# Attention scores of a fused conv and attention layer: the product with k low as two 64-row matmuls in the row halves of TensorE

## The reference

```python
qkv = conv1d_same(group_norm(xf, gn_gamma, gn_beta), qkv_w, qkv_b)   # 16 taps, 256 -> 768 channels, 1024 positions
qkv = qkv.reshape(b * NUM_HEADS, -1, t)                              # 4 batches x 4 heads, 64 channels each for q, k, v
w = jnp.einsum('bct,bcs->bts', q * scale, k * scale)                 # scores, 1024 x 1024 per head
w = jax.nn.softmax(w.astype(jnp.float32), axis=-1)
h = jnp.einsum('bts,bcs->bct', w, v)
h = conv1d_same(h, proj_w, proj_b)                                   # 5 taps, 256 -> 256 channels
```

## Time and profile before

| what | value |
|---|---|
| median of 3 runs | 1116.28 us (1116.11 to 1116.67) |
| profiled execution, device time | 1117.09 us |
| its span | 1115.3 us |
| mean granted TensorE clock | 0.965 of full speed |
| PE busy | 1000.0 us, 90% |
| DVE, ACT, POOL busy | 64%, 58%, 21% |
| score matmuls (L1114) | 512 |

### The profile page before, as it was taken

The page is one execution under the profiler, slowest core; times in us unless marked ns, Lnnn a source line. Parts: engine busy times, 40 slices in busy tenths (PEclk is TensorE's granted clock), DMA queues, the critical chain, the costliest instruction groups (busy, mean ns, idle before and its releaser), DMA issues.

```text
span 1115.3 us, 18112 instructions
## 1 busy us (share of the span) xinstructions
PE 1000.0 (90%) x7250; PEld 716.3 (64%) x7250; DVE 717.4 (64%) x1222; ACT 650.3 (58%) x1049; POOL 233.2 (21%) x164
## 2 busy tenths in 40 slices
PE   2887749999999999999598999999999999988864
PEld 1555526667766777667366666766677668766654
DVE  5988557663765477668466555464636665777767
ACT  4674627664666477757565656465636575665531
POOL 2736112100230142124050100010001004313320
PEclk9998869999999999999799999999999999999978
DMA  7040034583459357637644384437435873453522
GB/s 269 21 170 1 1 124 77 95 200 67 95 105 246 54 120 167 161 60 161 153 76 86 66 172 100 81 72 181 82 65 124 184 170 68 96 123 60 112 57 76
DMA packets 284515, 122.59 MB, mean 110 GB/s; under 512 B 268304, under 2 KB 270736, under 8 KB 283536
## 3 DMA queue, kind: packets, MB, share of 16 engines
q1 hardware_dynamic: 284432, 121.44, 48.5%
HBM read 34.24 MB, written 15.87 MB: 45 GB/s over the span
## 4 chain that ended last, share of the span: by engine, by line
PE 63%; DVE 10%; issue 7%; ACT 6%; POOL 1%; DMA 1%; SPq 0%; ACTq 0%; POOLq 0%; DVEq 0%
PE cQ L1049 15%; PE cM L1049 15%; PE cP L1049 14%; PE psV L1095 8%; PE psS L1114 4%; PE psT L1114 4%; DVE smx L1491 2%; ACT arena L909 2%; DMA arena<-arena 1%; PE cM L990 1%; DVE W L1276 1%; PE cP L990 1%; DVE arena L1468 1%; DVE W L1362 1%; ACT arena L921 1%
## 5 line engine op out<-in xcount | busy, mean ns | idle before, releaser
L1049 PE MATMUL cP<-U,W 128*128 128x256 f16 (+1 forms) x1536 | 224.1, 303 | 13.6 <-DVE W L1276 12.1
L1049 PE MATMUL cM<-U,W 128*128 128x256 f16 (+1 forms) x1536 | 222.9, 301 | 11.4 <-DVE U L1305 7.4
L1049 PE MATMUL cQ<-U,W 128*128 128x256 f16 (+1 forms) x1536 | 226.7, 303 | 5.7 <-DVE W L1276 3.5
L1049 PEld LDWEIGHTS cP<-U,W 128*128 128x128 f16 x1536 | 150.6, 98 | 81.7 <-issue 11.6
L1049 PEld LDWEIGHTS cM<-U,W 128*128 128x128 f16 x1536 | 149.4, 97 | 80.7 <-issue 8.5
L1049 PEld LDWEIGHTS cQ<-U,W 128*128 128x128 f16 x1536 | 150.7, 98 | 73.4 <-issue 5.1
L1468 DVE SCALAR_TENSOR_TENSOR arena<-arena,smx 128x1024 f16<-128x1024 f32 x128 | 179.0, 1398 | 1.3 <-ACT arena L921 0.5
L902 ACT ACTIVATE smx<-smx,esc 128x1 f32<-128x1 f32 x128 | 37.5, 293 | 212.8 <-DVE smx L1491 212.5
L921 ACT ACTIVATE arena<-arena,smx 128x1024 f16<-128x1024 f32 x128 | 147.0, 1148 | 4.2
L1095 PE MATMUL psV<-arena 128*128 128x256 f16 x1024 | 125.2, 276 | 12.0 <-DVE arena L1475 6.2
L1491 DVE TENSOR_REDUCE smx<-psS 128x1 f32<-128x1024 f32 x64 | 77.9, 1218 | 76.2 <-PE psS L1114 75.9
(11 more groups left out here) (210 smaller groups left out, 1142.2 us busy)
## 6 DMA issues: line engine op xcount, KB each, us to landing
staging<-w_qkv SPq DMA_DIRECT2D x20, 512.0 KB, 5.2
kept_u<-U SPq DMA_DIRECT2D x4, 2077.0 KB, 9.9
U<-kept_u SPq DMA_DIRECT2D x16, 519.2 KB, 4.3
arena<-x_tok SPq DMA_DIRECT2D x8, 512.0 KB, 6.4
arena<-arena SPq DMA_DIRECT2D x16, 256.0 KB, 3.8
W<-x_tok SPq DMA_DIRECT2D x4, 1024.0 KB, 6.1
out_tok<-W SPq DMA_DIRECT2D x3, 1024.0 KB, 4.3
kept_h<-arena SPq DMA_DIRECT2D x4, 514.0 KB, 4.5
```

What stands on the lines that cost most here:

```text
L1049: last = mm(out, W[:, j, wl, c, wat + tap, :], U[:, slot, ul, c, at:at + width], start=(c == 0 and tap == 0 and wl + ul == 0), stop=(c == ...
```

## The change

The (q high + q low) x k low product is replaced by q high x k low alone; q low x k low is left out of the computation. For each unit the first two matmuls stay (128 rows, k high). The other two now take 64 rows each: the first half of the keys uses q high and k low in partitions 0 to 63, the second half uses a copy of q high and k low in partitions 64 to 127. They write different PSUM banks.

```diff
-        sizes = (3 * T, T, 2 * HALF, 2 * T, 3 * T, 4 * T, HR // 2)
+        sizes = (7 * HALF, T, HALF, 2 * T, 3 * T, 4 * T, HR // 2)
...
+        heads = part[0].bitcast(F16).rearrange("p (h w) -> p h w", h=2)
+        stack = heads[:, :, 0:2 * T].rearrange("p h (k t) -> p h k t", k=2)
+        k_low, q_again = heads[:, :, 2 * T:2 * T + HALF], heads[:, :, 2 * T + HALF:]
...
-        hbuf = part[2].rearrange("p (q t) -> p q t", q=2)
+        hbuf = part[2]
...
-                sp.wait_ge(S["qk_lo"], 2 * (2 * k + hd + 1))
-                sp.dma_start(stack[0:D, hd, 1:3, :].rearrange("p k t -> p (k t)"),
-                             stack[D:P, hd, 1:3, :].rearrange("p k t -> p (k t)")).then_inc(S["qk_done"], 16)
+                sp.wait_ge(S["qk_lo"], 3 * (2 * k + hd + 1))
+                sp.dma_start(stack[0:D, hd, 1, :], stack[D:P, hd, 1, :]).then_inc(S["qk_done"], 16)
+                sp.dma_start(q_again[D:P, hd, :], stack[0:D, hd, 0, :]).then_inc(S["qk_done"], 16)
...
                 act.wait_ge(S["pv_done"], 8 * k + 2 * gi + 2)
-                a(hbuf[R:R + D, 0, :], psV[O:O + D, :], ACT.Copy, scale=2.0 ** -PROB_BITS).then_inc(S["ht_done"], 1)
+                wait(act, "hl_done", 4 * k + gi)
+                a(hbuf[R:R + D, :], psV[O:O + D, :], ACT.Copy, scale=2.0 ** -PROB_BITS).then_inc(S["ht_done"], 1)
...
                         if u % 8 == 0:
-                            pe.wait_ge(S["qk_done"], 16 * (2 * k + hd + 1))
+                            pe.wait_ge(S["qk_done"], 32 * (2 * k + hd + 1))
...
+                        scores, queries = (psS, psT)[u % 2], slice(u % 8 * P, (u % 8 + 1) * P)
                         for h in range(2):
-                            for l in range(2):
-                                last = mm((psS, psT)[u % 2][:, h * HALF:(h + 1) * HALF], stack[:, hd, 0, u % 8 * P:(u % 8 + 1) * P],
-                                          stack[:, hd, 1 + l, h * HALF:(h + 1) * HALF], start=(l == 0), stop=(l == 1))
+                            mm(scores[:, h * HALF:(h + 1) * HALF], stack[:, hd, 0, queries],
+                               stack[:, hd, 1, h * HALF:(h + 1) * HALF], start=True, stop=False)
+                        mm(scores[:, 0:HALF], stack[0:D, hd, 0, queries], k_low[0:D, hd, :], start=False, stop=True)
+                        last = mm(scores[:, HALF:T], q_again[D:P, hd, queries], k_low[D:P, hd, :], start=False, stop=True)
                         last.then_inc(S["s_done"], 1)
...
-                    v.scalar_tensor_tensor(stack[D:P, hd, 2, :], yqk[D:P, :], ysc[D:P, m, 0:1], stack[D:P, hd, 1, :],
+                    v.scalar_tensor_tensor(k_low[0:D, hd, :], yqk[D:P, 0:HALF], ysc[D:P, m, 0:1], stack[D:P, hd, 1, 0:HALF],
+                                           ALU.mult, ALU.subtract).then_inc(S["qk_lo"], 1)
+                    v.scalar_tensor_tensor(k_low[D:P, hd, :], yqk[D:P, HALF:T], ysc[D:P, m, 0:1], stack[D:P, hd, 1, HALF:T],
                                            ALU.mult, ALU.subtract).then_inc(S["qk_lo"], 1)
```

More of the change, by code:

```diff
@@ L81, in build @@
         part = [arena[:, edge[q]:edge[q + 1]] for q in range(len(sizes))]
-        stack = part[0].bitcast(F16).rearrange("p (h k t) -> p h k t", h=2, k=3)
+        heads = part[0].bitcast(F16).rearrange("p (h w) -> p h w", h=2)
+        stack = heads[:, :, 0:2 * T].rearrange("p h (k t) -> p h k t", k=2)
+        k_low, q_again = heads[:, :, 2 * T:2 * T + HALF], heads[:, :, 2 * T + HALF:]
         vT = part[1].bitcast(F16).rearrange("p (s h c) -> p s h c", s=8, h=2)
-        hbuf = part[2].rearrange("p (q t) -> p q t", q=2)
+        hbuf = part[2]
         prob = part[3].rearrange("p (q t) -> p q t", q=2)
@@ L88, in build @@
         Hr = part[6].bitcast(F16).rearrange("p (l r w) -> p l r w", l=2, r=2)
-        xs = arena[:, 0:edge[2]].rearrange("p (n i c) -> p n i c", n=2, i=8)
+        xs = arena[:, 0:4 * T].rearrange("p (n i c) -> p n i c", n=2, i=8)
         EO = CT * 2 * SEQW
@@ L580, in add_common @@
                 else:
-                    wait(pool, "qk_lo", 2 * (2 * n + j - 1))
+                    wait(pool, "qk_lo", 3 * (2 * n + j - 1))
                 y = yv if j == 0 else yqk
@@ L803, in heads_hi @@
                     act.wait_ge(S["hr_free"], 16 * (k + 1))
-                a(home(k)[R:R + D, 0, r, 1:1 + HALF], hbuf[R:R + D, 1, :], ACT.Copy).then_inc(S["hh_done"], 1)
+                a(home(k)[R:R + D, 0, r, 1:1 + HALF], hbuf[R:R + D, :], ACT.Copy).then_inc(S["hh_done"], 1)
             def main_copy(n, p, j):
@@ L1474, in heads_sum @@
                 dve.wait_ge(S["ht_done"], 4 * k + gi + 1)
-                v.scalar_tensor_tensor(hbuf[R:R + D, 1, :], psV[R:R + D, :], 2.0 ** -PROB_BITS, hbuf[R:R + D, 0, :],
+                v.scalar_tensor_tensor(hbuf[R:R + D, :], psV[R:R + D, :], 2.0 ** -PROB_BITS, hbuf[R:R + D, :],
                                        ALU.mult, ALU.add).then_inc(S["hs_done"], 1)
@@ L1482, in heads_low @@
                 dve.wait_ge(S["hh_done"], 4 * k + gi + 1)
-                v.tensor_tensor(home(k)[R:R + D, 1, r, 1:1 + HALF], hbuf[R:R + D, 1, :],
+                v.tensor_tensor(home(k)[R:R + D, 1, r, 1:1 + HALF], hbuf[R:R + D, :],
                                 home(k)[R:R + D, 0, r, 1:1 + HALF], ALU.subtract).then_inc(S["hl_done"], 1)
```

## The result

| | before | after |
|---|---|---|
| device time, median of 15 runs each | 1116.67 us (1115.66 to 1117.39) | 1119.27 us (1118.82 to 1120.62) |
| ratio to before, 95% interval | | 1.0025 [1.0017, 1.0033] |
| span of the profiled execution | 1115.3 us | 1118.8 us |
| mean granted clock | 0.965 | 0.952 |

The change makes the kernel slower by 0.25%, 2.6 us, where 9.4 us of gain was forecast. The page reads almost as before: TensorE is busy 4.7 us longer and has 64% of the chain for 63%; where the time went, these totals don't say.

A forecast was written before the change was run, and what follows sets the result against it. TensorE was taken to bound 98 of 128 units: -10.3 us from pair and switches, +0.9 us for copies, -9.4 us against 1117.09 us gives 1107.7 us, as a median 1106.9, rounded 1107 us; range 1095 to 1133 us.

The forecast's parts named there:

- What bounds the kernel: Whole kernel: TensorE's time counts in 98 units of scores and not in 30, in step 4 and the last step.
- The pair: Each unit's two 64-row matmuls run at the same time, so four passes become three: 215 ns less per unit.
- The switch: Two changes per unit between 128-row and 64-row use, 55 ns each; a unit wins 105 ns, 98 units 10.3 us.
- rival A: TensorE, each unit: the switch is free, 21.1 us less plus 0.9 for the copies, 1096 us; chance 0.19.
- the case that I gave 0.09: TensorE's units: pair serial with free switches, or 100 to 115 ns per switch cancel the gain; 1115 to 1119 us.
- A full exposed tail, 164 ns: TensorE empties at both switches of each unit, 328 ns against 215 gained; 1128 us; chance 0.20.
- one with an exposed load beside it (262 ns): Each switch also exposes the weight load: a unit loses 309 ns, 1147 us; chance 0.16, shared with a serial pair.
- My other sign of being wrong: TensorE, each unit: the forecast is wrong if the unit takes longer than 0.86 us.
- The copies: SP issues two DMAs of 128 KB for one of 256 KB: one extra issue at the start, +0.9 us.
- DVE's split: k low's subtraction in two: +93 ns sixteen times, 1.5 us of DVE, at most +0.4 us exposed, counted as 0.
- The last step keeps its length: The last step, from 934 to 1066 us, should keep its length of some 110 us.
- Step 4's stall: TensorE's 11.5 us stall in step 4 should change little or grow by about a microsecond.

The follow-up runs named there:

- the second profile: The changed kernel profiled once more, unedited: 1119.51 us, ratio 1.0020.
- joined everywhere: Changed kernel with each even unit's scores from unit 2 on issued together with the next unit's, four full matmuls then two pairs: 1125.11 us, ratio 1.0074.
- joined where there was slack: Changed kernel with GpSimd's wait; units issued in twos except 4, 5, steps 4 and 8, and units 6, 7 of steps 2 and 3: 1109.81 us.

## Why the prediction was wrong

**What bounds the kernel** was read rightly for small changes: 0.22 us more per unit came back as 23.9 us for 98 units (21.6). For a gain of 0.4 us per unit it fails: the kernel without the pair gains nothing over step 3, where a wait for DVE comes up.

**The pair: right.** It saves one pass of 215 ns. Starts 10 ns apart, and a second pair for 0.22 us.

**The switch: the failed step.** I priced it at 55 ns, "a third of the tail", and said that this was a choice. It is 105 ns on average of the two changes. That a change costs something was right, the size not: 98 x (215 - 2 x 105), some 0.4 us, stands where the sum had 10.3. That alone is 9.9 of the 12.4 us between the forecast of 1106.9 and the 1119.27 measured. The nearest row that I leaned on, the float32 transposes, keeps all 128 rows in use, and so says nothing on a change of rows. I had noted that against rival A and should have held it against my own value too. The true value lies within the case that I gave 0.09 (100 to 115 ns cancel the gain), a nanosecond or two short of the 107 from which the change is slower by TensorE alone. A full exposed tail, 164 ns, is ruled out by the paces, and so is one with an exposed load beside it (262 ns). An exposed load in place of the tail, 98 ns, was no case of mine; it is near the measured price, and the sign that I had named for it, idle weight loads before L1119 and behind L1120, is there. My other sign of being wrong, a unit of more than 0.86 us, did not come, and the forecast fails all the same: at 0.85 us the gain is already gone, so the sign was set too far out. The Trainium skill, "TensorEngine Tiling (Array Packing)", section "Key Properties", says that a change of mode drains TensorE. The runs agree that each change costs and that staying in the mode doesn't; that the 100 ns are a drain no run here shows.

**The copies: too dear.** +0.9 us forecast, nothing measured: TensorE starts 0.1 us earlier in one profile and 0.1 us later in the other.

**DVE's split: the second failed step.** "I count 0, ... +0.4 us at most" was wrong by an order: the kernel before with the split alone takes 3.9 us more. Of the 3.2 us by which its profiled span grew, 2.3 came with the split's collisions and 0.9 with the late clock. I took the mean price of the instruction, 93 ns for the cut, and passed over the largest of the sixteen, 4031 ns, that stood in the same row. An instruction of 1285 ns that once takes 4031 waits there for something, and what waits once in one piece can wait twice in two. The additions of GpSimd that it meets are 4.5 us long, and two stand back to back. The Trainium skill, "SBUF — State Buffer", section "SBUF: two separate sides", has the rule: the port pair that DVE and GpSimd share is held exclusively for a whole instruction, and a DVE operation with two inputs in SBUF needs it against a GpSimd operation that reads SBUF. The runs agree: 0.75 us free, 3.50 and 4.87 us against two additions, and 0.48 us undisturbed with one input in PSUM.

**ACT's new wait: right,** it holds nothing. **The last step keeps its length: wrong,** by the split: from its first scores to the end of the span it takes 1.8 us more, and its last scores come 3.4 us later. **Step 4's stall: right** in size (11.84 us for 11.52), though the step as a whole grew by 1 us, by the same collision.

**The clock: not foreseen.** 1.3 us are lost in the profiled execution where the clock rises later behind the first copy (0.9 us in the second profile). Its cause is open, and that it comes from the change isn't shown.

**The sum as measured** by the lags of the profiled executions: +1.2 (first units, with the clock), -0.5 (the lag shrinks between the other places), +1.0 (step 4), +5.2 less 3.4 given back (last step), in all +3.5, the difference of the spans. The medians differ by less, 2.6 us: the profiled execution after was the slowest of its fifteen runs, 1.35 us above their median.

## What to carry to other kernels

Matmuls over half of the rows that run in pairs save a pass, but each change to them or back costs about half a pass of 512 columns here: they paid only where several pairs stood behind one another and the reordering made no new wait. When an instruction is to be cut in two, look at its longest record and not at its mean; if it waits for another engine's whole instruction there, each piece may wait for one. After a gain on the busiest engine, see slot by slot which wait comes next: joined everywhere, the units lost 5.8 us to new waits; joined where there was slack, and with GpSimd's collision gone (4.0 us by itself), they won 9.5 us over the changed kernel.

## What the runs showed of the hardware

- A change from 128-row to 64-row use and back costs 211 ns at the full clock, two times about 105; the weight load at either border begins with its own matmul, not with the one before. A change between two 64-row matmuls on the same rows costs nothing (0.22 us for a further pair with its loads).
- The weight load of a 64 x 64 tile is recorded with 103 ns, that of 64 x 128 with 92 and of 128 x 128 with 98: half the columns did not halve it.
- A DVE operation with two inputs in SBUF that meets a running addition of GpSimd ends after it, by 0.55 us with 512 columns and by 1.08 to 1.10 us with 1024, and the next such operation waits for the next addition. In the same stretch DVE operations with an input in PSUM (0.48 us), or with one input (1.21 us), weren't held.
- The clock behind the same wait rose at different moments in kernels whose TensorE had nearly the same work (0.50 to 0.78 of full over the same 4 us), with up to 1.3 us of lag; the late rise went with a clock of 0.79 to 0.81 over the first 30 us, against 0.83 or 1.00. The changed kernel showed 0.50 both times.
